# Four-step score pieces in five more groups of a gated cross-attention kernel

## The reference

```
x = x + tanh(g_xattn) * attention(layernorm(x), ctx, ctx, mask, wq, wk, wv, wo)
x = x + tanh(g_ffn)   * expert_ffn(layernorm(x), route_w, A, Bw)      # top 1 of 8, rank 16
attention: q = x@wq (32 heads of 128), k, v = ctx@wk, ctx@wv (8 heads of 128, each shared by 4 query heads)
           rope on q and k; softmax(q k^T / sqrt(128) + mask); (p v) @ wo
```

## Time and profile before

| what | us |
|---|---|
| median of 3 runs | 1052.23 (1052.15 to 1052.72) |
| the profiled execution, its own time | 1052.35 |
| its span | 1050.5 |
| PE busy in the span | 1041.5 (99%) |
| DVE busy | 872.4 (83%) |
| ACT busy | 634.1 (60%) |
| POOL busy | 592.2 (56%) |

### The profile page before, as it was taken

How to read it: one execution, slowest core, us unless ns; L and a number is a source line. 1 busy time by engine, 2 the same in 40 slices (tenths; PEclk the granted TensorE clock), 3 DMA queues, 4 the chain that set the end, 5 groups by cost and what they waited for, 6 DMA issues and landing times.

```text
span 1050.5 us, 19132 instructions
## 1 busy us (share of the span) xinstructions
PE 1041.5 (99%) x6663; PEld 865.9 (82%) x6663; DVE 872.4 (83%) x1423; ACT 634.1 (60%) x1112; POOL 592.2 (56%) x518
## 2 busy tenths in 40 slices
PE   9999999999999999999999999999999999999998
PEld 7888888877788888888888888888888888888786
DVE  7875766788888888888888899878887878787997
ACT  7554466676767676767666645556564655555653
POOL 4552379887878787878764433334343434444423
PEclk9999999999999999999999999999999999999999
DMA  7768966475765656565469844464454545443102
GB/s 265 265 226 301 395 234 242 160 278 205 251 219 179 224 180 215 189 195 208 158 233 396 263 149 163 161 202 150 152 180 133 180 145 172 162 145 129 49 26 81
DMA packets 106094, 206.40 MB, mean 196 GB/s; under 512 B 8848, under 2 KB 58640, under 8 KB 100112
## 3 DMA queue, kind: packets, MB, share of 16 engines
q1 hardware_dynamic: 105424, 204.40, 56.6%
q10 hardware_dynamic: 576, 0.79, 0.2%
HBM read 122.31 MB, written 82.84 MB: 195 GB/s over the span
## 4 chain that ended last, share of the span: by engine, by line
PE 90%; DVE 5%; POOL 2%; issue 1%; ACT 1%; DMA 0%; SPq 0%; DVEq 0%; ACTq 0%
PE attn L998 31%; PE proj L925 27%; PE attn L867 8%; PE turned L867 4%; PE score L867 4%; PE score L947 3%; PE attn L983 3%; PE attn L985 3%; PE turned L958 3%; PE small L947 2%; PE proj L842 1%; DVE acc L1353 1%; PE proj L947 1%; DVE o_s L1341 1%; DVE stats L1206 1%
## 5 line engine op out<-in xcount | busy, mean ns | idle before, releaser
L998 PE MATMUL attn<-wo_s,o_s 128*128 128x512 f32 x1524 | 375.2, 395 | 0.6 <-DVE o_s L1341 0.5
L925 PE MATMUL proj<-xB,wq_s 128*128 128x512 f32 x1344 | 334.3, 391 | 0.0
L998 PEld LDWEIGHTS attn<-wo_s,o_s 128*128 128x128 f32 x1524 | 281.0, 188 | 58.5 <-DVE o_s L1341 1.4
L925 PEld LDWEIGHTS proj<-xB,wq_s 128*128 128x128 f32 x1344 | 251.6, 188 | 50.9
L1958 POOL TENSOR_TENSOR rot<-rot,tab 128x512 f32<-128x512 f32 x110 | 162.7, 1480 | 146.6 <-ACT rot L1677 146.4
L1241 DVE TENSOR_TENSOR q_r<-q_r,tab 128x512 f32<-128x512 f32 x127 | 114.4, 901 | 1.6 <-ACT x_third L1677 1.4
L1341 DVE TENSOR_TENSOR o_s<-attn,o_s 128x512 fp32r<-128x512 f32 x127 | 82.4, 685 | 32.4 <-ACT o_s L1726 32.4
L1698 ACT ACTIVATE copies<-proj 128x512 f32<-128x512 f32 x96 | 57.5, 599 | 81.1 <-PE proj L925 80.8
L1726 ACT ACTIVATE o_s<-attn 128x512 fp32r<-128x512 f32 x127 | 69.2, 597 | 57.3 <-PE attn L985 57.3
L1353 DVE SCALAR_TENSOR_TENSOR acc<-attn,gates_t,acc 128x512 f32<-128x512 f32 x127 | 94.9, 748 | 10.1 <-PE attn L998 7.7
L1958 POOL TENSOR_TENSOR rot_third<-rot_third,tab 128x512 f32<-128x512 f32 x40 | 61.6, 1541 | 57.4 <-ACT rot_third L1677 54.5
(11 more groups left out here) (277 smaller groups left out, 1735.3 us busy)
## 6 DMA issues: line engine op xcount, KB each, us to landing
wq_kept<-wq_s SPq DMA_DIRECT2D x16, 1792.0 KB, 6.4
wq_s<-wq_kept SPq DMA_DIRECT2D x16, 1792.0 KB, 8.1
v_kept<-vst SPq DMA_DIRECT2D x64, 256.0 KB, 4.5
v_s<-v_kept SPq DMA_DIRECT2D x128, 128.0 KB, 5.0
wo_kept<-wo_s SPq DMA_DIRECT2D x32, 512.0 KB, 6.5
wo_s<-wo_kept SPq DMA_DIRECT2D x32, 512.0 KB, 5.5
k_kept<-kst SPq DMA_DIRECT2D x32, 256.0 KB, 2.0
wq_raw<-in_wq SPq DMA_DIRECT2D x16, 512.0 KB, 7.9
```

What stands on the lines that cost most here:

```text
L925: last = e.matmul(dst[:, :], wq_s[:, b % 2, A, s, kt, :], xB[:, B, mv, kt, :], start=(first and kt == 0 and m == 0), stop=(kt == 1 and m = ...
L998: last = e.matmul(out_bank(k, bp)[:, :], o_s[:, s, bp, h, :], wo_s[n % WO_SLOTS][:, m, :], start=(h == 0 and i == 0), stop=(h == GROUP - 1 ...
```

## The change

Five more groups (2 to 6, steps 8 to 27) make their scores in a piece of four. With it, for first-half groups: product `first[:1]` of the third and fourth step of a group stands ahead of the values on PE and ACT; DVE makes both low halves of the probabilities together in the second step; POOL combines weights in the first step of a group behind `subtract_max` and behind `normalise` (two parts) as in other even steps; POOL's wo low half of the steps with k % 4 of 1 and 3 moves from the end of the step to behind the next step's `subtract_max`. On SP, in step 28, the last three x blocks are fetched ahead of a weight block and not behind it.

```
-QUADS = range(9, 15)
+QUADS = (*range(2, 7), *range(9, 15))

+def product_ahead(k):
+    return quad_begins(k) or in_quad(k) and k < HALF_STEPS and k % 4 >= 2
+def low_behind(k):
+    return in_quad(k + 1) and k + 1 < HALF_STEPS and k % 4 in (1, 3)

 SP:  -  if k % 2 == 0 and HEAD_PAIRS_ALL <= k // 2 + 3 < Q_BLOCKS:      (now behind fetch_xB)
      -      fetch_wq(k // 2 + 3)
         if k in (27, 28): ... fetch_xB(i)
      +  if k % 2 == 0 and HEAD_PAIRS_ALL <= k // 2 + 3 < Q_BLOCKS:
      +      fetch_wq(k // 2 + 3)
 PE, ACT:  first[:1] if quad_begins(k)  ->  if product_ahead(k)
 DVE: + lows_first = k % 4 == 1 and in_quad(k) and k < HALF_STEPS
      if not together:
      -    prob_low(k, 0)
      +    prob_low(k, *((0, 1) if lows_first else (0,)))
      ...  q_add of the step
      -prob_low(k, *((0, 1) if together else (1,)))
      +if not lows_first: prob_low(k, *((0, 1) if together else (1,)))
 POOL:
      -if quad_begins(k) and pieces:
      -    combine_weights(pieces[0][0])
       subtract_max(k)
      +for n in wo_late(k - 1) if low_behind(k - 1) else ():
      +    raw_low(("wo", n))
       ...
       elif k % 2 == 0 and pieces:
      -    if not quad_begins(k):
      -        combine_weights(pieces[0][0], (0,))
      +    combine_weights(pieces[0][0], (0,))
       ...
       normalise(k)
      -if k % 2 == 0 and pieces and not quad_begins(k):
      +if k % 2 == 0 and pieces:
           combine_weights(pieces[0][0], (1,) if k > 2 else (0, 1))
       ...
      -for n in wo_late(k) if k % 4 and k > 1 else ():
      +for n in wo_late(k) if k % 4 and k > 1 and not low_behind(k) else ():
           raw_low(("wo", n))
```

More of the change, by code:

```diff
@@ L804, in _ @@
                         store_wq(b)
-                if k % 2 == 0 and HEAD_PAIRS_ALL <= k // 2 + 3 < Q_BLOCKS:
-                    fetch_wq(k // 2 + 3)
                 if k in (27, 28):
@@ L809, in _ @@
                         fetch_xB(i)
+                if k % 2 == 0 and HEAD_PAIRS_ALL <= k // 2 + 3 < Q_BLOCKS:
+                    fetch_wq(k // 2 + 3)
                 if k % 4 == 2 and quad_begins(k + 2):
@@ L1109, in _ @@
                 between(k, 0)
-                for b, i in first[:1] if quad_begins(k) else ():
+                for b, i in first[:1] if product_ahead(k) else ():
                     product(b, i)
@@ L1113, in _ @@
                 between(k, 1)
-                for b, i in first[:1] if not quad_begins(k) else ():
+                for b, i in first[:1] if not product_ahead(k) else ():
                     product(b, i)
@@ L1519, in _ @@
                     add_mask(k + 2)
+                lows_first = k % 4 == 1 and in_quad(k) and k < HALF_STEPS
                 if not together:
-                    prob_low(k, 0)
+                    prob_low(k, *((0, 1) if lows_first else (0,)))
                 if quad_begins(k + 1):
@@ L1527, in _ @@
                 between(k, 6)
-                prob_low(k, *((0, 1) if together else (1,)))
+                if not lows_first:
+                    prob_low(k, *((0, 1) if together else (1,)))
                 add_out(k - 1, 1)
@@ L1792, in _ @@
                 between(k, 0)
-                for p in first if quad_begins(k) else ():
+                for p in first if product_ahead(k) else ():
                     copy_product(*p)
@@ L1800, in _ @@
                 between(k, 1)
-                for p in first if not quad_begins(k) else ():
+                for p in first if not product_ahead(k) else ():
                     copy_product(*p)
@@ L2005, in _ @@
                 pieces = weights_of(k)
-                if quad_begins(k) and pieces:
-                    combine_weights(pieces[0][0])
                 subtract_max(k)
+                for n in wo_late(k - 1) if low_behind(k - 1) else ():
+                    raw_low(("wo", n))
                 if k == 1:
@@ L2014, in _ @@
                 elif k % 2 == 0 and pieces:
-                    if not quad_begins(k):
-                        combine_weights(pieces[0][0], (0,))
+                    combine_weights(pieces[0][0], (0,))
                 elif k % 4 == 1:
@@ L2031, in _ @@
                     combine_weights(HEAD_PAIRS + 1, (1,))
-                if k % 2 == 0 and pieces and not quad_begins(k):
+                if k % 2 == 0 and pieces:
                     combine_weights(pieces[0][0], (1,) if k > 2 else (0, 1))
@@ L2052, in _ @@
                     weight_low(*pieces[1])
-                for n in wo_late(k) if k % 4 and k > 1 else ():
+                for n in wo_late(k) if k % 4 and k > 1 and not low_behind(k) else ():
                     raw_low(("wo", n))
```

## The result

The changed kernel takes 1062.24 us (median of 5, 1061.88 to 1062.88); the kernel before takes 1052.72 (median of 5, 1052.15 to 1053.11). The ratio is 1.009, with a 95% interval of 1.0078 to 1.0101: slower by 9.5 us, where 7.6 were forecast, inside the range.

What follows compares the result with a forecast made beforehand. PE was taken to bound the kernel, busy in 99% of the span. The terms -1.6 + 4.4 + 0.4 + 3.2 + 1.2 = +7.6 us on 1052.23 gave 1059.8 us, range 1053.8 to 1063.5.

Steps and rivals of the forecast that it cites:

- PE's saving: On PE in five groups: four steps' scores in one piece save 0.32 us a group, -1.6 us.
- First step: Group starts: POOL's low half and two combining pieces make the normalisation 0.90 us late; 5 x 0.88 = +4.4 us.
- Third step: The normalisation fits by 0.3 us before the weight load; 0.1 us taken for a tie, four times: +0.4.
- tie with the cosine product: Third step: DVE's first cosine product ties with POOL's normalisation; if DVE comes first, the stall is some 0.5 us.
- Fourth step: POOL's lateness is collected here and delays the normalisation: 0.8 us, bounds 0 and 1.6, four times: +3.2.
- The worked schedule: Fourth step, DVE and POOL taking turns: all that follows comes 1.5 us later, less 0.4 of slack: 1.1.
- Values of the fourth step: Values wait for DVE's low halves of the probabilities: 0.3 us, bounds 0 and 0.5, four times: +1.2.
- Edits at nothing: Product ahead, low halves together, SP queue and x blocks, all counted as costing nothing in the sum.
- x blocks: On SP: they go out 0.7 us earlier, the weight block behind them is due a step later: nothing.
- Low halves together: Second step: both low halves together have POOL's wait for a shift behind them: counted at nothing.
- Product ahead: Third and fourth steps: takes 1.36 us of cover between values and project_out; nothing, upper bound 0.1 to 0.3 a step.
- The SP queue: At group starts the moved wo head's store waits some 8 us longer, with loads queued behind it: counted at nothing.

Runs made afterwards that it cites:

- e3: The changed kernel with the fourth and second steps' wo low halves both made at the fourth step's end, behind DVE's last rope addition: 1055.24 us, ratio 1.0023.
- e9: e3 plus, in third steps, POOL's sine product ahead of the second combining part: 1054.97 us, ratio 1.0012.
- e2: e1 plus a POOL wait for DVE's last rope addition before the fourth step's wo low half: 1058.84 us, ratio 1.0063.
- e4: The changed kernel with the products of third and fourth steps back behind the values on PE and ACT: 1063.96 us.
- e5: The changed kernel with DVE's second low half of the probabilities behind the rope addition again in second steps of first-half groups: 1061.63 us.
- e10: The changed kernel with POOL's sine product ahead of the second combining part in third steps, nothing else: 1060.82 us.
- e12: The changed kernel with DVE's low halves of the probabilities ahead of the rope addition in fourth steps, nothing else: 1063.21 us.
- e7: The kernel before with three useless POOL instructions (512, 256, 256 elements) behind the subtraction at the six second-half group starts: 1055.81 us.
- e1: The changed kernel with the fourth step's wo low half back at the end of its step: 1059.93 us, ratio 1.0066.
- e11: e9 plus, in fourth steps, DVE's low halves of the probabilities ahead of the rope addition: 1055.06 us, ratio 1.0017.
- e8: The kernel before with only the x blocks of step 28 fetched ahead of the weight block: 1052.48 us.
- e6: The kernel before with one useless POOL instruction of 512 elements behind the subtraction at the six second-half group starts: 1053.57 us.

## Why the prediction came out

**PE's saving: right.** 16.44 + 10.96 + 12.33 + 10.95 = 50.68 holds in the first half too: e3 and e9 show second, third and (e9) fourth steps at these values, to 0.02. A first step of 16.44 was not seen there; the nearest are 16.50 (e9) and 16.51 (e2).

**First step: right, in place, cause and size.** Forecast 0.88 each, measured 0.80 at the first group start, where nothing else adds to it (17.24; in e4, e5, e10 and e12 it is 17.25 to 17.27). POOL and PEld of the changed kernel, step 12:

```profile
369.25 1.04 POOL L1977 TENSOR_TENSOR prob_even<-prob_even,neg_max 128x512 f32<-128x512 f32 x1 [5.91 <-DVE neg_max L1322]
370.25 1.30 POOL L1922 TENSOR_TENSOR wo_s<-raw,wo_s 128x512 fp32r<-128x512 f32 x1
...
371.51 0.74 POOL L1934 TENSOR_TENSOR combined<-wq_raw 128x256 f32<-128x256 f32 x1
...
372.21 0.73 POOL L1935 TENSOR_TENSOR combined<-wq_raw 128x256 f32<-128x256 f32 x1
...
372.91 1.04 POOL L1982 TENSOR_TENSOR prob_even<-prob_even,row_inv 128x512 f32<-128x512 f32 x1
...
374.00 0.42 PEld L968 LDWEIGHTS turned<-tab,prob_even 128*128 128x128 f32 x4 [1.01 <-POOL prob_even L1982]
```

The normalisation begins 372.91 - 369.25 = 3.66 after the subtraction; 3.64 was the sum from the earlier trace rows. At the first group start it is 320.01 - 316.36 = 3.65, so 0.91 late, and costs 0.80: the slack is 0.11, where 0.02 was allowed. By the figure of the Trainium skill (GPSIMD Engine Reference, section "Elementwise — side-by-side cycle accounting") the 3.66 would have been an estimated 3.2 and the stall an estimated 0.5. The trace does not agree: the low half took 1.30 and not 1.11, a combining piece 0.74 and not 0.55. e2 shows the cause by taking it away (17.24 to 16.51), e7 by making it elsewhere. One sentence of the forecast was too simple: that the idle time ahead of the subtraction "goes unused" suggests it was free. e1 and e2 show that for the first group start only its last part is, behind DVE's rope addition.

**Third step: no stall, 0.1 forecast.** The normalisation came first in its tie with the cosine product (343.10 against 343.23 in step 10), and all five third steps take 12.30 to 12.33. The 0.4 us of this term did not come.

**Fourth step: right in mechanism, the size in part by luck.** Forecast 0.8 each, measured 0.76, 0.74, 1.16 and 0.76. The trace has the schedule that the forecast worked out, POOL without idle from the low half on and then waiting for one rope addition; DVE and POOL take turns:

```profile
344.11 1.19 POOL L1938 TENSOR_TENSOR combined<-combined,wq_raw 128x256 f32<-128x256 f32 x1
345.38 1.07 POOL L1940 TENSOR_TENSOR combined<-wq_raw,combined 128x256 f32<-128x256 f32 x1
...
349.07 1.29 POOL L1945 TENSOR_TENSOR wq_s<-wq_raw,wq_s 128x512 fp32r<-128x512 f32 x1 [0.81 <-DVE q_r L1256]
...
355.03 1.04 POOL L1982 TENSOR_TENSOR prob_odd<-prob_odd,row_inv 128x512 f32<-128x512 f32 x1 [0.44 <-DVE row_inv L1333]
```

The weight low half begins 349.07 - 344.42 = 4.65 after step 10's transposes (forecast 4.8, in pairs 3.3). The normalisation of step 11 begins 355.03 - 344.42 = 10.61 after them and in pairs 453.76 - 444.48 = 9.28, so it is 1.33 later and costs 0.76: the slack is 0.57 and not 0.42. The worked schedule gave 1.1 and the 0.8 was a choice between it and nothing, which three groups bear out and the fourth, with 1.16, does not.

That such instructions shut each other out (the Trainium skill, SBUF — State Buffer, section "Who interferes with whom") agrees with 1.82 beside 1.30 in e2 and 0.68 beside 1.85 after. That issue order decides, as the same section says, these traces can't show: POOL's record begins 0.02 ahead in both cases. The tie that mattered is another than the one named, the sine against the cosine product of the fourth step. e3 and e9 show that this chain is the cause: with 1.25 us less on POOL the stall falls to 0.3, with the sine product also earlier it is gone. The last group has no such stall (10.97): its third step, 26, has no combining, as the forecast counted.

**Values of the fourth step: right place, half the size.** 0.3 was forecast; group starts after the first are 17.87, 0.63 over the first one. Changed kernel, DVE and PE, transposes of step 11 at 356.13:

```profile
359.77 1.18 DVE L1256 TENSOR_TENSOR q_r<-q_r,rot 128x512 f32<-128x512 f32 x1
...
360.87 1.40 DVE L1343 TENSOR_TENSOR p_low<-turned,p_high 64x512 fp32r<-64x512 f32 x2
```

```profile
362.37 0.47 PE L993 MATMUL attn<-p_high,v_s 128*128 128x256 f32 x2
...
363.11 0.51 PE L993 MATMUL attn<-p_high,v_s 128*128 128x256 f32 x2
```

The low halves end at 362.27, 6.14 after the transposes (slack was said to end at 5.7), and PE starts at 362.37. The forecast counted this one wait. There is a second: values start in two pairs, 0.74 apart and not 0.47 as without a stall, because the second waits for the output sum behind the low halves. e11 separates them: with the low halves early, the second wait alone costs 0.77 (there the output sum begins 6.27 after the transposes, in the changed kernel 6.17). And the whole is not tied to the fourth step's stall as thought: e9 has no stall there and still loses 0.5. What decides is whether step 11's normalisation has slack (0.42 in the pairs of the earlier trace rows, none in e9); that is argued from the traces and was not tried by itself.

**Edits at nothing.** x blocks: nothing (e8). Low halves together: nothing (e5). Product ahead: worth 0.4 a group (e4). The SP queue, 8 us later at group starts, held nothing up that a trace shows.

**Sum.** -1.6 + 4.0 (0.8 x 5) + 0 + 3.4 + 2.5 (0.63 x 4) + 0.2 = 8.5 in the groups, against 7.6; the rest of the measured 9.5 is not located in the change. Part of this closeness is luck: first and third steps came 0.8 lower than forecast in all, the values 1.3 higher.

## What to carry to other kernels

Before filling an engine's idle time on a nearly slackless chain, add up the gap: here 1.70 us between two POOL instructions took 1.4 us of work for almost nothing (0.07 in e2), and 2.7 us cost PE 0.8. Idle time is only free where the other engine on the same path does not need what the filler takes; a wait on the last such instruction of that engine (e2) gave the filler a place that cost nearly nothing at group starts. When a stage is made shorter on the bound engine (2.2 us of scores gone from the third step), recount the work of every other engine in that step: the lateness showed one step later.

## What the runs showed of the hardware

A tie of 0.02 us for what POOL and DVE share moves a fourth step by 0.43 us (11.70 or 12.13). It falls to POOL in all four groups of e2, in three of four of e1 and in one of four of the changed kernel, to DVE in the others.

Unexpected too: in a piece of four steps' scores PE now and then stops in a row of independent matmuls, with nothing to wait for in the profile, for 0.15 to 0.71 us in the first half (in the profiles of after, e1, e3, e4, e5, e9 and e10; twice in e9; not in e2, e11 and e12), in none of the second half's pieces in any profile, and in none of the pairs of the kernel before, e6, e7 and e8. Where POOL's work is not what PE waits for next, the group start grows by more than the gap shown: 17.70 beside 17.13 for 0.30 in e3, 17.99 beside 16.95 for 0.71 in e9. What DMAs move at the time is not the reason: they moved 4 GB/s around the stop of 0.59 in e5 (365 to 369 us), and 358 GB/s in the scores of step 16 of the kernel before (409.1 to 411.1 us), where PE did not stop. The cause stays open.
